# Query projection by seven half products instead of eight, in a cross-attention and router kernel

## What is computed

```
scores = q k^T / sqrt(128), masked; attn = softmax(scores)
x = x + concat(attn v) @ Wo
```

## Time and profile before

| | us |
|---|---|
| median of 3 runs | 624.38 |
| profiled execution | 623.29 |
| its span | 621.5 |

### The profile page before, as it was taken

How to read it: one execution, slowest core, us unless ns; L and a number is a source line. 1 busy time by engine, 2 the same in 40 slices (tenths; PEclk the granted TensorE clock), 3 DMA queues, 4 the chain that set the end, 5 groups by cost and what they waited for, 6 DMA issues and landing times.

```text
span 621.5 us, 10479 instructions
## 1 busy us (share of the span) xinstructions
PE 603.3 (97%) x3076; PEld 506.1 (81%) x3076; DVE 420.9 (68%) x730; ACT 347.1 (56%) x1008; POOL 323.7 (52%) x342
## 2 busy tenths in 40 slices
PE   9999999899999999999999999999999999999895
PEld 7887888688888888888888888888888888888673
DVE  5565667687667766776676667667766676668884
ACT  5222555485566556655655575557555755574543
POOL 6340778765338434843574366436643763374321
PEclk9999999999999999999999999999999999999996
DMA  8820141211003100310040003001200210000011
GB/s 286 283 61 8 35 119 52 68 35 36 0 1 103 34 1 1 101 34 0 0 118 17 0 17 101 17 0 34 84 17 0 61 40 0 0 2 2 34 49 54
DMA packets 16025, 29.58 MB, mean 48 GB/s; under 512 B 2048, under 2 KB 2176, under 8 KB 16000
## 3 DMA queue, kind: packets, MB, share of 16 engines
q1 hardware_dynamic: 15472, 28.22, 14.7%
q0 software_dynamic: 384, 1.05, 0.5%
q10 hardware_dynamic: 144, 0.00, 0.0%
HBM read 27.17 MB, written 2.10 MB: 47 GB/s over the span
## 4 chain that ended last, share of the span: by engine, by line
PE 86%; DVE 5%; POOL 4%; issue 2%; ACT 2%; DVEq 0%; ACTq 0%; POOLq 0%
PE proj L980 10%; PE proj L982 10%; PE proj L981 10%; PE outp L1126 9%; PE outp L1128 9%; PE outp L1127 8%; PE score L1081 8%; PE probT L1094 4%; PE attnT L980 2%; PE outp L980 2%; PE outp L982 2%; PE attnT L982 2%; PE outp L981 2%; PE attnT L981 2%; POOL rot L367 2%
## 5 line engine op out<-in xcount | busy, mean ns | idle before, releaser
L573 ACT ACTIVATE probs<-score,negmax 128x128 f32<-128x128 f32 x256 | 90.3, 366 | 61.2 <-DVE negmax L808 61.2
L367 POOL TENSOR_TENSOR rot<-rot,sinT 128x512 f32<-128x512 f32 x80 | 106.9, 1336 | 29.1 <-ACT rot L505 29.1
L504 ACT ACTIVATE rot<-proj 64x512 f32<-64x512 f32 x72 | 42.7, 594 | 125.1 <-PE proj L982 125.0
L800 DVE SCALAR_TENSOR_TENSOR score<-score,mask_bias 128x512 f32<-128x512 f32 x64 | 44.7, 698 | 97.3 <-PE score L1081 97.3
L411 POOL TENSOR_TENSOR probs<-probs,rsum 128x512 f32<-128x512 f32 x64 | 66.6, 1040 | 83.0 <-DVE rsum L814 83.0
L1126 PE MATMUL outp<-wo_hi,oT_hi 128*128 128x512 f32 x256 | 107.2, 419 | 2.6 <-DVE oT_lo L843 2.3
L1128 PE MATMUL outp<-wo_hi,oT_lo 128*128 128x512 f32 x256 | 100.8, 394 | 0.0
L980 PE MATMUL proj<-xT_hi,wq_hi 128*128 128x512 f32 x256 | 100.2, 391 | 0.0
L1127 PE MATMUL outp<-wo_lo,oT_hi 128*128 128x512 f32 x256 | 100.0, 391 | 0.0
L982 PE MATMUL proj<-xT_hi,wq_lo 128*128 128x512 f32 x256 | 99.7, 390 | 0.0
L981 PE MATMUL proj<-xT_lo,wq_hi 128*128 128x512 f32 x256 | 99.7, 389 | 0.0
(11 more groups left out here) (161 smaller groups left out, 1150.7 us busy)
## 6 DMA issues: line engine op xcount, KB each, us to landing
ring_a<-in_wq SPq DMA_DIRECT2D x32, 256.0 KB, 2.5
ring_b<-in_wo SPq DMA_DIRECT2D x32, 256.0 KB, 2.5
ctx_in<-in_ctx SPq DMA_DIRECT2D x8, 256.0 KB, 4.2
ring_b<-in_wv SPq DMA_DIRECT2D x8, 256.0 KB, 7.1
resid<-in_x SPq DMA_DIRECT2D x2, 1024.0 KB, 13.2
ring_a<-in_wk SPq DMA_DIRECT2D x8, 256.0 KB, 2.7
out<-ff_out SPq DMA_DIRECT2D x8, 256.0 KB, 2.0
mask_in<-in_mask SPq DMA_DIRECT2D x1, 512.0 KB, 13.3
```

The source lines that it names most:

```text
L367: pool.tensor_tensor(rot[:, k0 % 2, :], rot[:, k0 % 2, :], sinT[:, half * W:(half + 1) * W], ALU.mult).then_inc(sin_done, 1)
L573: last = act.activation(probs[:, p, h, :], heads(score[p][:, :])[:, h, :], ACT.Exp, bias=negmax[:, p, h:h + 1], accum_out=sums[:, p, h:h + 1])
L800: dve.scalar_tensor_tensor(heads(score[p][:, :]), heads(score[p][:, :]), SCALE, mask_bias[:, b, :].unsqueeze(1).broadcast_to([P, GH, S]), ...
```

## The change

**The products.** Two query heads (a pair: heads r and r+2 of a group), two feature halves (2 chunks each) and two token halves make a 2x2 by 2x2 block product. Before it was eight half products of 6 matmuls a pair and two token halves (four units of 12). Now seven, `m1` to `m7`, of sums of weight blocks (`S1` to `S4`, made in `w_sum` by POOL) and sums of x blocks (`T1` to `T4`, made once at the start by POOL). There are 16 pairs. The four results are C11, C12, C21, C22 (head by token half):

Cut to its core:

```diff
 # SP
+            for i in range(KB * B):
+                store_v(i)
+                if i in (B + 2, B + 4):
+                    load_wk(RA + (i - B) // 2 - 1)
+            for i in range(VS):
+                sp.wait_ge(dma_vout[i], 16 * len(range(i, KB * B, VS)))
+            for half in range(NH):
+                load_v(0, half)
+            for r in range(WK, KV):
+                load_wk(r)
+                for k in (2 * (r - WK) + 2, 2 * (r - WK) + 3):
+                    store_k(k)                     # waits rope_done >= k + 1
+            load_pair(0, 0, first=True)
+            for k in range(KV + 2, KK):
+                store_k(k)
+                if k == 3 * KV // 2:
+                    load_pair(1, 0)
+            for i in range(KS):
+                sp.wait_ge(dma_kout[i], 16 * len(range(i, KK - NH, KS)))
 # ScalarE, key units k
+                if half == NH - 1 and g + WK < KV:
+                    hi_wk(g + WK)
+                if k in (0, 2, 4):
+                    hi_x((B11, B21, B22)[k // 2], False)
+                if k in (8, 9, 10, 11):
+                    hi_x((T1, T2, T3, T4)[k - 8], True)
+                if 9 <= k < 9 + PIECES:
+                    hi_w((W0, W3, W1, W2)[k - 9], 0, 0)
+                if k >= 14:
+                    hi_w((W0, W3)[k - 14], 1, 0)
 # DVE, key units k (after times_cos and add_rotated)
+                if half == NH - 1 and g + WK < KV:
+                    dve.wait_ge(k_hi, r + 1)
+                    dve.tensor_tensor(wk_lo[:, r % WK], ...)
+                if 8 <= k < 15:
+                    lo_x((B11, B21, B22, T1, T2, T3, T4)[k - 8], k - 7)   # 1024 columns
 # DVE, ahead of the queries
+            for i in range(KS):
+                dve.wait_ge(dma_kout[i], 16 * len(range(i, KK - NH, KS)))
 # POOL: sum_x(k) (512 columns) after rotate for k < 8; sums and lo parts of pair 0, 1 for k >= 9
 # POOL, main loop
+                if b not in (0, 4) and not last:
+                    rotate((Q0 + b, g, B), ROPE_HALF[b])
+                if b in (0, 1):
+                    lo_wo(g, 2 * b)
+                    lo_wo(g, 2 * b + 1)
+                if lead and not last:
+                    p = (4 if b < 5 else 5)
+                    if b in (2, 5):  sums12(p, g); lo_w(W0, p, g)
+                    if b in (3, 6):  sum3(p, g); sum4(p, g); lo_w(W3, p, g)
+                    if b in (4, 7):  lo_w(W1, p, g); lo_w(W2, p, g)
+                if b == 3: lo_v(g, 1)
+                if b == 6 and not last: lo_v(g + 1, 0)
+                if b in (0, 4) and not last:
+                    rotate((Q0 + b, g, B), ROPE_HALF[b])
 # ScalarE, main loop, after the exponentials: hi_w in b 4, 7; keep_s, keep_t, keep_u; then
+                if b == 0 and not last:
+                    swap_c21(2, Q0, g)
+                if b == 4 and not last:
+                    swap_c21(3, Q0 + b, g)
                 act.wait_ge(pv_done, n + 1)
                 act.activation(oT_hi[:, :], attnT[:, :], ACT.Copy).then_inc(ot_hi, 1)
+                if b == 0:
+                    for h in range(GH):
+                        if not first:
+                            act.wait_ge(o_done, n * GH - GH + h + 1)
+                        hi_wo(g, h)
 # TensorE step: after the transposes m4(2) m1(3) m6(3) m7(3) m4(3) m1(4) m6(4) m7(4) in b = 0..7,
 # then output(b-1) and the attention product, and after that
+                    if b == 0: m3(2, g)
+                    if b == 1: m2(3, g)
+                    if b == 3: m5(3, g)
+                    if b == 4: m3(3, g)
+                    if lead:
+                        if b == 5: m2(4, g)
+                        if b == 7: m5(4, g)
```

More of the change, by code:

```diff
@@ L484, in _ @@
             for b in range(B):
-                step(0, b, first=True)
-            with pool.Fori(1, KV - 1) as g:
+                step(0, b)
+            with pool.Fori(1, KV - 2) as g:
                 for b in range(B):
                     step(g, b)
+            for b in range(B):
+                step(KV - 2, b, lead=False)
             for b in range(B):
@@ L601, in _ @@
[L601 to L620 removed]
+            act.wait_ge(dma_vout[VS - 1], 16 * len(range(VS - 1, KB * B, VS)))
@@ L867, in step @@
                 if last:
                     ffn(b, 0)
-                if not (first and b == 1):
-                    lo_p(n)
+                lo_p(n, first and b == 0)
                 if ahead:
                     row_max(b % 2, n + FIRST + 1)
-                if query:
-                    rope_query(b + AHEAD - 1, g, 1)
-                accumulate((b - 1) % B, n, first)
+                if last and b == 0:
+                    rope_query(None, 1, Q0, g, 1, 1)
+                if not last and b in ROPES:
+                    rope_query(None, head, Q0 + b, g, half, 1)
@@ L876, in step @@
+                if not (first and b == 0):
+                    accumulate((b - 1) % B, n, first, last and b > 0)
                 if last:
@@ L879, in step @@
                     invert_sums(b % 2, n + FIRST + 1)
-                lo_o(n)
+                if not last:
+                    if b == 0:
+                        dve.wait_ge(proj_free, U_K + Q0 + g * B)
+                        times_cos(bank_a[:, :], Q0, g, B, hold[:, 3, :], 0)
+                    if b == 4:
+                        times_cos(bank_a[:, :], Q0 + 4, g, B, qT[:, 0, 3, :], 0)
+                lo_o(n, first and b == 0)
                 if last:
@@ L1073, in scores @@
-            def scores(b0, g, first=False):
+                three(early_bank(u)[:, :], [(wk_hi[:, g % WK, c, :], wk_lo[:, g % WK, c, :],
+                                             ctxT_hi[:, c, cols], ctxT_lo[:, c, cols]) for c in range(C)]).then_inc(proj_done, 1)
+            def scores(b0, g, first=False, last=False):
                 p, b = b0 % 2, b0 % B
-                half = b0 // HB
-                pe.wait_ge(rope_done, KV * NH + (half + 1) * GH + g * B)
+                half, group = b // HB, b0 // B
+                pe.wait_ge(rope_done, KK + (half + 1) * GH + (half if not last else 0) + group * B + g * B)
@@ L1086, in step @@
+            def step(g, b, first=False, lead=True, last=False):
                 n = b + g * B
                 if not (last and b + FIRST >= B):
-                    scores(b + FIRST, g)
+                    scores(b + FIRST, g, last=last)
                 pe.wait_ge(soft_done, n + 1)
```

1042 lines of the change are left out of this document (699 added, 343 removed).

## The result

The changed kernel takes 711.34 us (median of 4 runs, 708.80 to 711.99) against 624.21 us (623.13 to 624.38) for the kernel before, measured beside it: a ratio of 1.139, 95% interval 1.137 to 1.142. It is slower by 14%, in the direction forecast, but above the range (630 to 706) and 37 us above the forecast of 674.

What follows compares the result with a forecast made beforehand. TensorE was taken to set the loop's time, with hand-overs from other engines deciding: 623.29 - 21.8 + 40 + 22 + 7 + 2.5 = 673.0, with 1.1 for the median 674 us; range 630 to 706.

Steps and rivals of the forecast that it cites:

- signs foretold: Profile after: output idle 4 to 7 us a group, group 61.5 to 64, first query product 120 to 126, ring_a waits.
- Wo hand-over: Step 1 of each group: TensorE waits for POOL's new Wo low parts, 5.0 us each; +40 us, ends 35 and 55.
- key stage: Key units: loads queued behind key stores delay the first query products; +22 us, ends 10 and 28.
- Unfilled steps: Steps 5 to 7 of group 6 and step 0 of the last lose their products; +2.5 us, ends 0 and 5.
- It must stand **4.4 us: Output of step 1: TensorE's wait before the fourth head, POOL's chain 10.4 us against 6.0 of TensorE work.
- first products: Ahead of the loop: nineteen half products feed one another through ACT copies and wait; +7 us, ends 2 and 14.
- removed: All 16 pairs: 96 matmuls fewer at 0.2275 us each, -21.8 us in all.
- Only the Wo hand-over: Rival: only the loop's wait for Wo binds, the keys' lateness hides in four banks; about 640 us, chance 0.17.
- only the start: Rival: POOL makes its low parts earlier, the loop runs at 57.3 us a group; 631 us, chance 0.10.
- DVE is the bound: Rival: in the loop port waits add up, a group of 64 us or more; about 702 us, chance 0.13.
- second SBUF operand: DVE's six cosine products a group reading `hold`: 0.5 us more each, near 1.2 us.
- Faster: Rival: POOL parts fall in gaps, hand-over under 1 us a group, start under 5; about 615 us, chance 0.09.

Runs made afterwards that it cites:

- b_wo_late: Kernel before, with only the change's late making of the Wo high and low parts (groups 1 to 7): 665.61 us, ratio 1.067.
- a_wo4: Changed kernel with Wo parts made as before: high parts ahead of the exponentials, four low parts together in step 0: 670.16 us, ratio 1.075.
- a_fill: Changed kernel plus 19 unused matmuls where TensorE stands before the third head of output, step 1 of groups 0 to 6: 703.44 us, ratio 1.128.
- a_first: Changed kernel with only ScalarE's order ahead of the loop changed, part_t and part_u of pair 2 earlier: 704.74 us, ratio 1.130.
- a_all3: a_all2 with the first pT_lo taken by VectorE right after the second reciprocal, ahead of the rotary additions: 644.18 us, ratio 1.035.
- a_keys: Changed kernel with only SP's order changed, key-stage loads moved ahead of key stores: 692.05 us, ratio 1.110.
- a_all4: a_all3 with TensorE's single wait for all x low parts split, and x parts made in order of use: 645.04 us, ratio 1.035.
- a_all2: Changed kernel with a_wo4, a_keys and a_first together, plus probabilities' low part ahead of rotary work in steps 1 and 5: 644.72 us, ratio 1.035.
- a_keys_xcopy: a_keys with x_lo written as x_raw times zero (one SBUF operand, low part of x left out): 688.77 us, ratio 1.106.

## Why the prediction was right and wrong

**What was right: the places and the waits.** The signs foretold were there: `wo_lo` as releaser once a group, key units behind `ring_a`, DVE at 46.9 us a group, 96 matmuls fewer; the group (65.3, not 61.5 to 64) and the first half product (132.94, not 120 to 126) came later than told. The group of before was read short, too, as eight times one step of 7.50 us (60.0), where whole groups lie 60.46 apart. The forecast summed 71.5 us of waits (40 + 22 + 7 + 2.5); TensorE is idle 75.0 us more. The Wo hand-over was read to the instruction: POOL's order in 8.95 us (9.36 measured), the stand 4.4 us (3.88 to 4.55 in the first seven groups, 4.4 in the mean), 35 us in all, since the last group has 4.2 in three pieces. It was put at 5.0, as between ScalarE in time and late; ScalarE was 0.4 us late (`oT_hi` at 254.46, 0.7 us after the attention product was issued at 253.78, where 0.29 was in time), and only the head was another, the third and not the fourth. That it is caused by the move alone is shown by b_wo_late. In the key stage the queue of loads behind stores is as told, ending on the `ring_a` waits; waits there grew by 25 us (26.0 against 0.95) where 22 had been taken (the prediction's own reading, 125 less 100.65, would have been 24). Unfilled steps idle some 1.6 us, less than the 2.5.

**The step that failed** is the price of a stand. The hand-over was costed as "It must stand **4.4 us**", and everything behind it at 0.2275 us a matmul; so were key stage and first products. After each of the seven stands the 15 matmuls to the next scores run at a granted clock of 0.52 to 0.58 and take 2.4 to 2.9 us more than their 3.41, so a hand-over costs 4.4 + 2.6 = 7.0 us in the mean in place of 5.0. Slow matmuls come to 35.5 us over the kernel (some of it the small gaps of a_wo4), and the span misses its forecast by 39: 35.5, and 3.5 of waits. That standing is the cause is shown for the loop by a_fill, with clock 1.00 once TensorE has work; for the start, where the clock is 0.85 and 0.83 in the two stages, it is read from the rows and not tested. The stretches read of the kernel before ran at clock 1.00, so none of the rows taken showed this price, and the text neither bounded it nor said that it was left out. The trace had it to show, in its last 9.5 us, where the router's matmuls lie between waits of 0.4 to 1.6 us:

```profile
612.00:621.50 9.50, 4.05 (x12) 2.32 (x11) 3.26 (x13) 2.23 (x6) 0.69 (x3) 0.50 0.22 83
```

The Trainium skill (TensorE: Matmul & The Clock Gate, Part 1) says that a TensorE left idle between bursts of matmuls falls back to half its clock; the trace agrees, with 0.54 behind the stand of 4.43 us in group 1.

By stage, with the clock in it, the first two terms lie over their upper ends and the third at its own. The keys are the 32.3 us by which the first half product is late. The first products are 56.9 - 28.6, less 6.8 for 21 half products where there were 8 units. The hand-over and the unfilled steps are what is left in the loop and the tail: 520.4 us from step 1 to the end against 492.3, plus the 28.6 us of matmuls (21.8 + 6.8) that no longer lie there:

```
                 predicted (ends)   measured   of it idle   of it slow
keys                22 (10 to 28)      32.3        25           7
first products       7 (2 to 14)       21.5        14           8
Wo hand-over        40 (35 to 55)      55          35          20
unfilled steps      2.5 (0 to 5)        1.6         1.6           0
removed          -21.8               -21.8
```

Idle and slow of the first two rows are from TensorE's busy time in the two stages; in the loop they are from the waits and good to some 2 us. The columns add up to 88.6, 75.6 and 35, against 88.7, 75.0 and 35.5 from the page.

**First products, +7.** This is the one term whose waits were read far too small: 16.1 us, less 2.28 before. The cause was named only in part. The wait for `part_t` behind the exponentials was put at 3 and is 3.63, that of pair 0 at 3 and is 0.28, but the first attention product was given 2 us and had 7.45. a_first (7.24 with `pT_hi` early) and a_all3 (2.09 with `pT_lo` moved) show that most of it was DVE's order, behind the rotary additions.

**The rivals.** "Only the Wo hand-over" and "only the start" fell: b_wo_late and a_keys each show their part alone. "DVE is the bound" gave 702, nearest in time, and fell too: with the hand-over put back a group is 59.6 us, DVE is busy 45.0, and what it delays is 1.35 us. Its second SBUF operand was priced right: the cosine product from `hold` took 1117 ns in the mean (1.2 foretold), 681 from PSUM. The Trainium skill's rule (SBUF — State Buffer, Who interferes with whom) that a DVE instruction with two SBUF inputs and a GpSimd one that reads SBUF exclude each other agrees in kind with `x_lo` at 1.2 to 2.3 us; what POOL's work adds in the loop is half a microsecond an instruction in the mean, not a whole POOL instruction. "Faster" needed the last low part within 1.5 us and m1 before 106. In a_all4 m1 starts at 102.89 and the hand-over is in time, and yet the kernel is 3.5% slower: the point from which it should decide was badly chosen, because the products that follow m1 have their own suppliers.

**What the change is worth at its best here.** It removes 21.8 us of matmuls, of which the small gaps of a_wo4, for which the prediction had no term, take back some 5 (an estimate, 7 groups at 0.75 us). In the best order examined stage by stage (a_all2), 16 of the 28.6 that fall in the loop and tail are kept, and the start costs 37 more (6.8 of it products moved there). No version ran faster than the kernel before; whether another order of DVE and POOL in the start can win back 21 us was not tried.

## What to carry to other kernels

Cost a stand of TensorE, where it sets the time, as the stand plus the slow matmuls behind it, and check the sum with two numbers of the page, span less busy time and busy time against the count of instructions. When a change gives its partner engines more to do, write down for each hand-over the order of the supplier's instructions, and keep the producer of the next group's operands in one piece ahead of everything that can wait. A wait that is split or moved is worth nothing if the same supplier is late at each of the pieces.

## What was not expected of the hardware

After 3.9 to 4.6 us without a matmul TensorE ran 11 to 13 matmuls slowly (the first 0.59 us, the others 0.43) before 0.2275 came back, in the first seven groups (granted clock 0.52 to 0.58 over the 5.8 to 6.4 us behind the stand). In b_wo_late the same stand of 3.98 us was followed in three hand-overs by 14 slow matmuls (clock 0.61 over 7.76 us) and in three by about 7, which began 0.3 to 0.6 us behind the stand (0.75 over 6.73): the price of a stand was not the same each time. Short waits, close together, kept it low for 17 us (a_all4, 108.5 to 125) at less idle in sum (10.2 us) than one long wait (13.5 us). And the DVE instruction of a_keys_xcopy, with a single SBUF operand (680 ns for 1024 columns beside an idle POOL), also stretched to 1233 and 1751 ns while POOL was at work.
